# Four graph-network layers on one core: copies, first products, activations and update products of the dense stage moved one round apart, masks of the running sums in 16 bit

## The chip, the cores and the metric

The kernel runs on one core of a Trainium2 chip. The metric is the device time of one execution in microseconds (us). The program is written by hand: each engine (TensorE, ScalarE, VectorE, GpSimdE and SyncE; PE, ACT, DVE, POOL and SP in the profile) has its own stream of instructions and waits on semaphores.

## What is computed

`x` is 100000 x 96 in fp32, there are 50000 edges sorted by `dst`, and four layers follow each other, each as `x = x + layer(relu(layernorm(x)))`. Cut to what matters:

```python
# layer 0 (edges touch only some nodes; for every node:)
update = gelu(concat(h, aggregated) @ uW1 + ub1) @ uW2 + ub2
x = x + layernorm(h + update) * ln_g + ln_b
# layer 1
x = x + relu(concat(h, m) @ Wu1 + bu1) @ Wu2 + bu2
# layer 2: segment mean of (h[src] @ W + b) by dst
# layer 3: three normalised graph convolutions of h, each relu(m @ W + b)
```

`aggregated` and `m` are sums of messages over the edges that end in a node. They are zero for most nodes.

## The kernel before

The work is done in stages, one after another: tables of the edges (0 to about 509 us), the **dense stage**, the edge stage of layer 0 (e0), that of layer 1 (e1), and four convolution stages (conv 0 to 3). The dense stage computes layers 0 and 1 for all nodes as if they had no edges. The later stages correct the nodes that have some.

**Dense stage.** It works on 196 groups of 512 nodes (`NG`). `pipelined(engine, n, stages)` (L107) writes the loop of each engine: in round i it calls each listed function with the group i minus the function's lag, in the order of the list. The lag is the number behind each name. All engines execute their own list strictly in order, but PE may load weights early. What follows is the path of one group, with lines:

- SP loads 512 rows of `x` into `xd`. DVE `mom_x` takes their moments (L1207, `mv<-xd`).
- DVE `roots` (L1160 to L1182, eleven small instructions) turns the moments of three groups at three places of the path into `rstd` and `nmr`. It is the last of each DVE round, and one such batch serves three readers on ACT: `norm1` (this round's new group), `norm_y` and `norm2` (older groups).
- ACT `norm1` writes `hd` (L701, four instructions). PE `tr1` (L895) transposes it into PSUM bank 0. ACT `evac1` (L746) copies that to `hdT`. PE `z1` (L888, `bank<-hdT,uw`) writes the first product to bank 1. ACT `gelu1` (L751) writes `u1`. PE `out1` (L908 and L909, 16 instructions in all) adds the update to the group in PSUM.
- DVE `mom_y` (L1207, `mv<-bank`) takes the moments of that PSUM bank, ACT `norm_y` (L736) normalises it into `yg`, DVE `times_g` (L1226), `plus_x` (L1234) and `plus_b` (L1239) make the new row `xn`, and `mom_z` (L1207, `mv<-xn`) takes its moments.
- ACT `norm2` writes `hs` (L701), PE `tr2` (L916) transposes it into bank 3, ACT `evac2` (L757) copies it, PE `z2` (L888, `bank<-hsT,wu`) makes the first product of layer 1 in bank 4, ACT `relu2` (L762) writes `v1`, PE `out2` (L928) the update product, DVE `finish_x` (L1251) and `finish_o` (L1258) the results.

Banks 0, 1, 3 and 4 are single. So `z1` of group j waits for `gelu1` of group j - 1, and `z2` for `relu2` of the group before. `out1` and `out2` alternate between two banks each.

**Running sums.** In e0, e1 and the convolution stages DVE adds messages along the sorted edges with `tensor_tensor_scan` (L1293): the carry is multiplied by a mask `goes`, 1 where an edge has the same `dst` as the one before and 0 elsewhere. SP loads the mask of 512 edges from DRAM, the same for every partition (L504, L535).

**Queues.** In the e and conv stages POOL gathers rows with indirect DMAs (L610), eight or four instructions for each group of 512 edges. In the dense stage it gathers four small pieces in each round (`got`).

Of the kernel before, what the change touches and what calls it, by code (L numbers as in the profile page):

```python
# [6 lines left out]
F16 = mybir.dt.float16  # L7
I32 = mybir.dt.int32
# [3 lines left out]
P = 128  # L12
# [5 lines left out]
GE = G * P  # L18
EG = 98
ET = EG * G  # L20
E_PAD = EG * GE
NG = (N + GE - 1) // GE
# [3 lines left out]
HI, LO = 128, 784  # L26
# [24 lines left out]
def need(eng, count, value):  # L51

    sem, base = (count.sem, count.base) if isinstance(count, Count) else (count, 0)
    if not isinstance(value, int) or value > 0:
        eng.wait_ge(sem, value + base)  # L55
# [41 lines left out]
def pipelined(eng, n, stages):  # L97


    most = max(stage[1] for stage in stages)  # L100
    last = max([n + most] + [stage[2] for stage in stages if len(stage) > 2])
    first = (most + 2 * UNROLL - 1) // UNROLL * UNROLL
    turns = (n - 1 - first) // UNROLL

    def step(g):
        for stage, lag, *always in stages:
            if g.turn is not None or (always and g.c < always[0]) or (not always and 0 <= g.c - lag < n):  # L107
                stage(g.shift(-lag))

    for i in range(first):  # L110
        step(Group(None, i))
    with eng.Fori(0, turns) as turn:  # L112
        for c in range(UNROLL):
            step(Group(turn, first + c))
    for i in range(first + turns * UNROLL, last):
        step(Group(None, i))


def build(nc, a, out):
    with ExitStack() as ctx:  # L120
        def sb(name, shape, dt=F32):
            return ctx.enter_context(nc.sbuf_tensor(name, shape, dt))
# [4 lines left out]
        def dram(name, shape, dt=F32):  # L127
            return nc.dram_tensor(name, shape, dt, kind="Internal").ap()
# [1 line left out]

        srcp = dram("srcp", (E_PAD,), I32)
        dstp = dram("dstp", (E_PAD + 2,), I32)
        goes_d = dram("goes_d", (E_PAD,))
        info_d = dram("info_d", (HI * LO, 2))
        t1 = dram("t1", (E_PAD + N, D))
        t2 = dram("t2", (E_PAD + N + E_PAD, D))
# [28 lines left out]
        st_s = sb("st_s", [P, ET], I32)  # L165
        st_d = sb("st_d", [P, ET], I32)
        st_p = sb("st_p", [P, ET], I32)
        st_goes = sb("st_goes", [P, ET])
        edge_pad = sb("edge_pad", [1, 2], I32)
        blk_i = sb("blk_i", [LB, 3, 4, P], I32)  # L170
        cols = sb("cols", [P, 3, ET])
# [23 lines left out]
        hd = sb("hd", [P, 6, G, D])  # L195
        mv = sb("mv", [P, 3, 3, G, 3])
# [17 lines left out]
        v1 = g1  # L214
        per_deg = sb("per_deg", [P, 2, G])
        msg = sb("msg", [P, 2, G, D + 1])
        goes = sb("goes", [P, 3, GE])
        iota_lo_i = goes[:, 0:2, :].rearrange("p s e -> p (s e)")[:, 0:LO].bitcast(I32)
        tanh_g = sb("tanh_g", [D, 2, GE])
        msgT = sb("msgT", [D, 2, GE])  # L220
        drop = sb("drop", [P, 3, G, D])
# [6 lines left out]
        xo = sb("xo", [P, 3, G, D])  # L228
        oo = sb("oo", [P, 3, G, D])
        degi, cum = (xn[0:HI, :, :, :].rearrange("p s c d -> p (s c d)")[:, i * LO:(i + 1) * LO] for i in range(2))  # L230
        has, home = (b[0:HI, :, :, :].rearrange("p s c d -> p (s c d)")[:, 0:LO] for b in (xo, oo))
        dego = hd[0:HI, :, :, :].rearrange("p s c d -> p (s c d)")[:, 0:LO]

        bank = [ctx.enter_context(nc.psum_tensor(f"bank{i}", [P, 512], F32)) for i in range(8)]

        def tok(b, w=D):

            return b[:, 0:G * w].rearrange("p (a c) -> p a c", c=w)
# [40 lines left out]
        def Phase(n, counts, slots):  # L279

            made = {}
            for name, per in counts.items():
                made[name] = so_far(name)
                passed[name] = made[name].base + n * per
            for name, (many, dmas, each) in slots.items():
                made[name] = []
                for k in range(many):
                    made[name].append(so_far(f"{name}{k}"))  # L290
                    passed[f"{name}{k}"] += ended((n + each - 1) // each, many, k, dmas)
            return made

        def more(name, k, by):
# [3 lines left out]
        dn = Phase(NG, dict(norm=1, mx=1, my=1, mz=1, t1=1, r1=1, z1=1, g1=1, u1=1, yx=1, xr=1, x1=1, t2=1, r2=1, z2=1,  # L298
                            g2=1, u2=1, fin=1, oo=1, norm2=1, norm_y=1),
                   dict(x_in=(6, 1, 1), x1_out=(6, 1, 1), x2_out=(3, 1, 1), o_out=(3, 1, 1), idx_in=(2, 1, GT),  # L300
                        got=(2, 2 * GI * GT, GT), kept=(2, 1, GT)))
# [394 lines left out]
        def _(act):  # L696
# [33 lines left out]
            def standard(ph, g, y, lag, q):  # L730

                b = g.shift(lag).at(3)
                need(act, ph["root"], ROOT * (g.j + lag + 1))
                need(act, ph["yx"], g.j - 1)
                for c in range(G):
                    ins = nc.scalar.activation(yg[:, g.at(2), c, :], y[:, c, :], ACT.Identity,  # L736
                                               bias=nmr[:, b, q, c:c + 1], scale=rstd[:, b, q, c:c + 1])
                ins.then_inc(ph["norm_y"].sem, 1)

            def norm_y(g):  # L740
                standard(dn, g, tok(bank[2 + 4 * g.at(2)]), 2, 1)

            def evac1(g):
                need(act, dn["t1"], g.j + 1)
# [19 lines left out]

            act.wait_ge(const_step, 1)
            act.wait_ge(weights_in, 16 * n_weights[0])
            pipelined(act, NG, [(gelu1, 1), (relu2, 5), (norm1, 0), (norm2, 4), (norm_y, 2), (evac1, 0), (evac2, 4)])

            for ph in (e0, e1):
                first = ph is e0  # L770
# [85 lines left out]
        def _(pe):  # L856
# [76 lines left out]
            pe.wait_ge(table_step, 7)  # L933
            pe.wait_ge(const_step, 1)
            pe.wait_ge(idx_step, 1)
            pipelined(pe, NG, [(out1, 1), (out2, 5), (tr1, 0), (tr2, 4), (z1, 0), (z2, 4)])

            need(pe, dn["fin"], NG)
            for ph in (e0, e1):
# [100 lines left out]
        def _(dve):  # L1040
# [106 lines left out]
            def pair_stats(x, into):  # L1147

                for c in range(0, G, 2):
                    ins = nc.vector.bn_stats(into[:, c:c + 2, :].rearrange("p c f -> p (c f)"),  # L1150
                                             x[:, c:c + 2, :].rearrange("p c d -> p d c"))
                return ins
# [34 lines left out]
            def roots_of(ph, readers):  # L1187

                def of_round(g):
                    b = g.at(3)  # L1190
                    roots(mv[:, b, :, :, :].rearrange("p q c f -> p (q c) f"),
                          steps + (rstd[:, b, :, :].rearrange("p q c -> p (q c)"), nmr[:, b, :, :].rearrange("p q c -> p (q c)")),
                          readers(g), ph["root"], ROOT * g.j)
                return of_round

            def upto(g, n, *counts):

                return [(count, value if g.turn is not None else min(value, n)) for count, value in counts]

            def wide(row):  # L1200

                return row.unsqueeze(1).broadcast_to([P, G, D])
# [14 lines left out]
            def mom_y(g):  # L1217
                need(dve, dn["u1"], g.j + 1)
                dve.sem_inc(dve_turn, 1)
                pair_stats(tok(bank[2 + 4 * g.at(2)]), mv[:, g.shift(2).at(3), 1, :, :]).then_inc(dn["my"].sem, 1)  # L1220

            def times_g(ph):
                def times(g):
                    need(dve, ph["norm_y"], g.j + 1)
                    dve.sem_inc(dve_turn, 1)
                    nc.vector.tensor_tensor(yx[:], yg[:, g.at(2), :, :], wide(rows[:, 0, :]), ALU.mult)\  # L1226
                        .then_inc(ph["yx"].sem, 1)
                return times
# [30 lines left out]
                    .then_inc(dn["oo"].sem, 1)  # L1259

            def dense_state(g):
                return upto(g, NG, (dn["norm"], g.j - 2), (dn["norm_y"], g.j - 4), (dn["norm2"], g.j - 6),
                            (dn["mx"], g.j + 1), (dn["my"], g.j - 1), (dn["mz"], g.j - 3))

            dve.wait_ge(info_out, 16)
            pipelined(dve, NG, [(times_g(dn), 4), (finish_x, 7), (plus_x, 4), (finish_o, 7), (plus_b, 4), (mom_x, 0),
                                (mom_y, 2), (mom_z, 4), (roots_of(dn, dense_state), 0, NG + 4)])
            for s in range(3):
                need(dve, dn["x2_out"][s], ended(NG, 3, s))
                need(dve, dn["o_out"][s], ended(NG, 3, s))  # L1270
# [213 lines left out]
```

## Time and profile before

| | us |
|---|---|
| median of 3 runs | 6881.36 (6865.93 to 6893.16) |
| the profiled execution's own time | 6877.96 |
| its span, first to last instruction | 6876.1 |
| PE busy | 4438.8 (65%) |
| DVE busy | 3951.5 (57%) |
| ACT busy | 3522.4 (51%) |
| POOL busy | 4259.0 (62%) |

No engine is busy all the time, since the stages have different limits. The busy shares are therefore to be read for each stage, and in a stage by the rounds of its loop: how long a round takes, and which wait ends last in it.

### The profile page before, as it was taken

The page shows a single profiled execution, that of the slowest core. Times are in us where ns is not written, and L with a number is a line of the kernel's source. Part 1 is how long each engine was busy: PE and PEld are TensorE (multiplying, and loading weights), DVE is VectorE, ACT ScalarE, POOL GpSimd, SP SyncE. Part 2 cuts the span into 40 slices and gives each one's busy share as a digit, 9 for nine tenths or more (in the row PEclk, how much of TensorE's full clock was granted, in tenths as well). Part 3 has the DMA queues.
Part 4 walks back from the last instruction along what each step waited for, and adds up shares of the span by engine and source line. Part 5 has one row for each costly group of instructions (what it writes and reads, how often), then busy time and mean ns, then how long its engine had stood idle before and what let it go on. Part 6 is the DMA issues. An engine that isn't in the chain of part 4 may idle for free. (4 is left out here: it accounts for less than half of the span.)

```text
span 6876.1 us, 104878 instructions
## 1 busy us (share of the span) xinstructions
PE 4438.8 (65%) x19614; PEld 2908.5 (42%) x19614; DVE 3951.5 (57%) x12722; ACT 3522.4 (51%) x8822; POOL 4259.0 (62%) x4323
## 2 busy tenths in 40 slices
PE   5768888888886777776887776554555555322222
PEld 2225566555663333333444443444444444222222
DVE  5667777777775666665555554666666344322222
ACT  6987887888885776775555553222222222111110
POOL 0005454555546777775777776775775776677777
PEclk9998988999887888887888887555555555555555
DMA  0003333333332333332444444665554899433332
GB/s 16 0 5 85 102 102 97 102 102 102 102 98 73 77 78 75 76 75 68 118 119 116 119 118 103 161 160 141 123 129 120 119 126 127 79 76 78 79 84 66
DMA packets 958039, 652.70 MB, mean 95 GB/s; under 512 B 730453, under 2 KB 834785, under 8 KB 957946
## 3 DMA queue, kind: packets, MB, share of 16 engines
q1 hardware_dynamic: 819962, 483.05, 25.0%
q0 software_dynamic: 137984, 168.67, 16.2%
q8 instruction: 27, 0.44, 0.0%
q14 instruction: 66, 0.54, 0.0%
HBM read 420.24 MB, written 232.62 MB: 95 GB/s over the span
## 5 line engine op out<-in xcount | busy, mean ns | idle before, releaser
L610 POOL DMA_INDIRECT got<-info_d,idx x784 | 776.8, 991 | 1258.6 <-issue 732.5
L610 POOL DMA_INDIRECT xs<-t,idx x1176 | 1110.8, 945 | 502.4 <-issue 347.7
L1031 PE MATMUL bank<-w,aggT 96*128 96x96 f32 (+1 forms) x3136 | 773.9, 428 | 470.5 <-DVE aggT L1293 470.4
L1024 PE MATMUL bank<-ident,msg 128*96 128x128 f32 (+1 forms) x1568 | 424.3, 426 | 991.3 <-ACT msg L848 819.7
L1031 PEld LDWEIGHTS bank<-w,aggT 96*128 96x128 f32 (+1 forms) x3136 | 703.5, 329 | 581.8 <-issue 500.7
L610 POOL DMA_INDIRECT xs<-c,idx x784 | 748.3, 954 | 314.9 <-issue 233.1
L848 ACT ACTIVATE msg<-xs,now 128x96 f32<-128x96 f32 x784 | 229.3, 363 | 1297.3 <-DMA xs<-c,idx 679.3
L1024 PEld LDWEIGHTS bank<-ident,msg 128*96 128x96 f32 (+1 forms) x1568 | 290.1, 218 | 1052.0 <-ACT msg L848 678.8
L1293 DVE TENSOR_TENSOR_SCAN aggT<-goes,aggT,bank 96x512 f32<-96x512 f32 (+1 forms) x490 | 621.2, 1268 | 135.0 <-DMA goes<-goes_d 63.1
L701 ACT ACTIVATE hd<-xd,nmr,rstd 128x96 f32<-128x96 f32 x1568 | 599.1, 454 | 27.0 <-DVE nmr L1182 27.0
L610 POOL DMA_INDIRECT xs<-in_x_dram,idx x392 | 473.3, 1207 | 173.9 <-issue 119.2
L1207 DVE BATCH_NORM_STATS2 mv<-xs 128x6 f32<-128x192 f32 x392 | 122.9, 355 | 752.4 <-DMA xd<-in_x_dram,idx 353.9
L1435 DVE SCALAR_TENSOR_TENSOR y<-bank,now,rows 128x96 f32<-128x96 f32 x392 | 97.3, 311 | 702.3 <-PE bank L1031 702.3
L687 POOL DMA_INDIRECT out_dram<-xn,idx_out x392 | 390.4, 996 | 119.4 <-issue 119.1
L610 POOL DMA_INDIRECT xd<-in_x_dram,idx x392 | 386.8, 987 | 119.4 <-issue 119.4
L610 POOL DMA_INDIRECT xd<-t,idx x392 | 370.0, 944 | 119.4 <-issue 119.4
L1435 DVE SCALAR_TENSOR_TENSOR xn<-bank,now,rows 128x96 f32<-128x96 f32 x784 | 194.5, 311 | 395.1 <-PE bank L1031 358.6
L875 PE MATMUL bank<-xd,hot_hi 128*128 128x392 f16 x1568 | 324.8, 329 | 124.0 <-ACT hot_hi L713 115.7
L949 PE MATMUL bank<-ident,hs 128*128 128x128 f32 (+1 forms) x784 | 151.4, 325 | 376.3 <-ACT hs L701 374.8
L701 ACT ACTIVATE hs<-xs,nmr,rstd 128x96 f32<-128x96 f32 x784 | 300.3, 455 | 174.0 <-DVE nmr L1182 173.8
L1093 DVE TENSOR_SCALAR xd<-iota_lo,lo_of 128x784 f16<-128x784 f16 x784 | 297.0, 421 | 143.6 <-PE bank L875 143.5
L888 PE MATMUL bank<-hdT,uw 96*96 96x512 f32 x392 | 249.1, 721 | 179.2 <-ACT hdT L746 179.2
(189 smaller groups left out, 10722.2 us busy)
## 6 DMA issues: line engine op xcount, KB each, us to landing
goes<-goes_d SPq DMA_DIRECT2D x392, 256.0 KB
t<-xo SPq DMA_DIRECT2D x392, 192.0 KB, 3.5
t<-xn SPq DMA_DIRECT2D x294, 192.0 KB, 2.3
xd<-in_x_dram SPq DMA_DIRECT2D x196, 192.0 KB, 2.4
out_dram<-oo SPq DMA_DIRECT2D x196, 192.0 KB
goes<-goes_d SPq DMA_DIRECT2D x196, 192.0 KB
xd<-t SPq DMA_DIRECT2D x196, 192.0 KB, 4.0
c<-xn SPq DMA_DIRECT2D x196, 192.0 KB, 3.7
```

What stands on the lines that cost most here:

```text
L610: nc.gpsimd.indirect_dma_start(out=into, out_offset=None, in_=table, in_offset=bass.IndirectOffsetOnAxis(ap=indices, axis=0)).then_inc(don ...
L687: nc.gpsimd.indirect_dma_start(out=out[:, :], out_offset=bass.IndirectOffsetOnAxis(ap=idx_out[:, half(g), col + c:col + c + 1], axis=0), i ...
L701: ins = nc.scalar.activation(into[:, c, :], x[:, c, :], ACT.Relu, bias=nmr[:, b, q, c:c + 1], scale=rstd[:, b, q, c:c + 1])
L848: ins = nc.scalar.activation(msg[:, g.at(2), c, 0:D], xs[:, g.at(6), c, :], ACT.Relu, scale=scale[:, col + c:col + c + 1])
L875: ins = nc.tensor.matmul(bank[1 + 2 * which + side][0:HI, 0:SIDE], hot_hi[:, g.at(2), which, 0:HI], hot_lo[:, g.at(2), which, side * SIDE: ...
L888: nc.tensor.matmul(into, w, x, start=True, stop=True).then_inc(done.sem, 1)
L949: ins = nc.tensor.transpose(bank[0][0:w, c * P:(c + 1) * P], hs[:, g.at(3), c, 0:w], ident[:])
L1024: ins = nc.tensor.transpose(bank[g.at(2)][0:m, c * P:(c + 1) * P], msg[:, g.at(2), c, 0:m], ident[:])
L1031: ins = nc.tensor.matmul(tok(bank[2 + g.at(2)], m)[:, c, :], aggT[0:m, g.at(3), c * P:(c + 1) * P], w2[:] if k == 0 else w3[:, k - 1, :], ...
L1093: nc.vector.tensor_scalar(hot_lo[:, g.at(2), which, :], iota_lo[:], lo_of[:, which, bass.ds(g.j, 1)], None, ALU.is_equal).then_inc(hot, 1)
L1293: nc.vector.tensor_tensor_scan(aggT[0:m, s, :], goes[0:m, s, :], source(g), aggT[0:m, before, GE - 1:GE], ALU.mult, ALU.add)\
L1435: ins = nc.vector.scalar_tensor_tensor(out=to, in0=u[:, c, 0:D], scalar=now[:, half(g), 1, col + c:col + c + 1], in1=rows[:, 1 + k, :], op ...
```

## The change

In the dense stage `evac1`, `z1`, `evac2` and `z2` are called one round later than before (lags 1 and 5, which were 0 and 4), and so are `gelu1`, `out1`, `relu2` and `out2` (lags 2 and 6, which were 1 and 5). `mom_y` and `norm_y` have lag 3, which was 2. `norm1`, `tr1`, `norm2`, `tr2`, `times_g`, `plus_x`, `plus_b`, `mom_z` and `finish_x` keep their lags. Each engine's list is put in another order too. Apart from the dense stage, the mask is kept in 16 bit, in DRAM and in SBUF, and the integers from which a constant is made lie in another buffer, since the mask's has become too small.

```diff
-        goes_d = dram("goes_d", (E_PAD,))
+        goes_d = dram("goes_d", (E_PAD,), F16)
...
-        st_goes = sb("st_goes", [P, ET])
+        st_goes = sb("st_goes", [P, ET], F16)
...
-        goes = sb("goes", [P, 3, GE])
-        iota_lo_i = goes[:, 0:2, :].rearrange("p s e -> p (s e)")[:, 0:LO].bitcast(I32)
+        goes = sb("goes", [P, 3, GE], F16)
...
+        iota_lo_i = hd[:].rearrange("p s c d -> p (s c d)")[:, 1024:1024 + LO].bitcast(I32)
...
-                standard(dn, g, tok(bank[2 + 4 * g.at(2)]), 2, 1)
+                standard(dn, g, tok(bank[2 + 4 * g.at(2)]), 3, 1)
...
-            pipelined(act, NG, [(gelu1, 1), (relu2, 5), (norm1, 0), (norm2, 4), (norm_y, 2), (evac1, 0), (evac2, 4)])
+            pipelined(act, NG, [(evac1, 1), (evac2, 5), (gelu1, 2), (relu2, 6), (norm_y, 3), (norm1, 0), (norm2, 4)])
...
-            pipelined(pe, NG, [(out1, 1), (out2, 5), (tr1, 0), (tr2, 4), (z1, 0), (z2, 4)])
+            pipelined(pe, NG, [(z1, 1), (z2, 5), (out1, 2), (out2, 6), (tr1, 0), (tr2, 4)])
...
-                pair_stats(tok(bank[2 + 4 * g.at(2)]), mv[:, g.shift(2).at(3), 1, :, :]).then_inc(dn["my"].sem, 1)
+                pair_stats(tok(bank[2 + 4 * g.at(2)]), mv[:, g.shift(3).at(3), 1, :, :]).then_inc(dn["my"].sem, 1)
...
-                return upto(g, NG, (dn["norm"], g.j - 2), (dn["norm_y"], g.j - 4), (dn["norm2"], g.j - 6),
-                            (dn["mx"], g.j + 1), (dn["my"], g.j - 1), (dn["mz"], g.j - 3))
+                return upto(g, NG, (dn["norm"], g.j - 2), (dn["norm_y"], g.j - 5), (dn["norm2"], g.j - 6),
+                            (dn["mx"], g.j + 1), (dn["my"], g.j - 2), (dn["mz"], g.j - 3))
...
-            pipelined(dve, NG, [(times_g(dn), 4), (finish_x, 7), (plus_x, 4), (finish_o, 7), (plus_b, 4), (mom_x, 0),
-                                (mom_y, 2), (mom_z, 4), (roots_of(dn, dense_state), 0, NG + 4)])
+            pipelined(dve, NG, [(finish_x, 7), (mom_y, 3), (finish_o, 7), (mom_x, 0), (times_g(dn), 4), (plus_x, 4),
+                                (plus_b, 4), (mom_z, 4), (roots_of(dn, dense_state), 0, NG + 4)])
```

How the instructions stand on ACT, in a steady round of the dense stage, before:

```order
L701 ACTIVATE hd<-xd,nmr,rstd 128x96 x4
L701 ACTIVATE hs<-xn,nmr,rstd 128x96 x4
L736 ACTIVATE yg<-bank,nmr,rstd 128x96 x4
L746 ACTIVATE hdT<-bank 96x512
L757 ACTIVATE hsT<-bank 96x512
L751 ACTIVATE u<-bank,bias 96x512
L762 ACTIVATE g<-bank,bias 96x512
```

And with the change (the first row is the first of a round here):

```order
L746 ACTIVATE hdT<-bank 96x512
L757 ACTIVATE hsT<-bank 96x512
L751 ACTIVATE u<-bank,bias 96x512
L762 ACTIVATE g<-bank,bias 96x512
L736 ACTIVATE yg<-bank,nmr,rstd 128x96 x4
L701 ACTIVATE hd<-xd,nmr,rstd 128x96 x4
L701 ACTIVATE hs<-xn,nmr,rstd 128x96 x4
```

`norm_y` (L736) has moved ahead of `norm1` and `norm2` (L701). The copies, which before stood behind the norms of their own groups, now serve the groups that were transposed a round earlier, and the norms end the round. On PE the order around the ring is the one of before (`z1`, `z2`, `out1`, `out2`, `tr1`, `tr2`), only for other groups.

On DVE, in a steady round of the dense stage, before:

```order
L1182 SCALAR_TENSOR_TENSOR nmr<-mv,rstd 128x12
L1226 TENSOR_TENSOR yx<-yg,rows 128x384
L1251 TENSOR_TENSOR xo<-xn,bank 128x384
L1234 TENSOR_TENSOR xn<-yx,xd 128x384
L1258 TENSOR_TENSOR oo<-xo,relu_b 128x384
L1239 TENSOR_TENSOR xn<-xn,rows 128x384
L1207 BN_STATS mv<-xd 128x6 x2
L1207 BN_STATS mv<-bank 128x6 x2
L1207 BN_STATS mv<-xn 128x6 x2
L1160 TENSOR_SCALAR var<-mv 128x12
```

And with the change:

```order
L1182 SCALAR_TENSOR_TENSOR nmr<-mv,rstd 128x12
L1251 TENSOR_TENSOR xo<-xn,bank 128x384
L1207 BN_STATS mv<-bank 128x6 x2
L1258 TENSOR_TENSOR oo<-xo,relu_b 128x384
L1207 BN_STATS mv<-xd 128x6 x2
L1226 TENSOR_TENSOR yx<-yg,rows 128x384
L1234 TENSOR_TENSOR xn<-yx,xd 128x384
L1239 TENSOR_TENSOR xn<-xn,rows 128x384
L1207 BN_STATS mv<-xn 128x6 x2
L1160 TENSOR_SCALAR var<-mv 128x12
```

`finish_x` (L1251) and `mom_y` (L1207, `mv<-bank`), the two that read what PE wrote, have moved to the head of the round. `times_g`, `plus_x`, `plus_b` and `mom_z`, each of which reads what the one before wrote, now stand next to each other.

## Rows read from the trace of the kernel before

**Rows 1.** Windows (us; busy PE, PEld, DVE, ACT, POOL; clock; DMA; GB/s): dense stage, e1.

```profile
565.10:2089.00 1523.90, 1285.90 (x6923) 905.44 (x6921) 1161.14 (x4238) 1251.36 (x3074) 745.35 (x752) 0.88 0.33 101
...
3270.00:4240.00 970.00, 774.62 (x3484) 454.79 (x3483) 508.40 (x1720) 517.26 (x1154) 714.35 (x757) 0.87 0.47 117
```

**Rows 2.** Instructions that write `oo` (min/median/max ns, first and last start).

```profile
L1258 DVE TENSOR_TENSOR oo<-xo,relu_b x196: 544/551/558, 565.1 to 2089.0; 128x384 f32<-128x384 f32 x196
```

**Rows 3.** Timeline of PE, one dense round (start us, us, name, idle before).

```profile
1523.72 1.10 PE L888 MATMUL bank<-hdT,uw 96*96 96x512 f32 x2 [1.12 <-ACT hdT L746]
1524.66 1.02 PE L888 MATMUL bank<-hsT,wu 96*96 96x512 f32 x2
1525.59 0.46 PE L908 MATMUL bank<-uw,u 97*128 97x96 f32 x2
...
1527.45 1.06 PE L928 MATMUL bank<-wu,g 97*128 97x96 f32 x8
1528.35 0.60 PE L895 MATMUL bank<-ident,hd 128*96 128x128 f32 x4
1529.31 0.64 PE L916 MATMUL bank<-ident,hs 128*96 128x128 f32 x4 [0.36 <-ACT hs L701]
1531.07 1.10 PE L888 MATMUL bank<-hdT,uw 96*96 96x512 f32 x2 [1.12 <-ACT hdT L746]
```

**Rows 4.** Timeline of ACT, the same round.

```profile
1524.86 0.68 ACT L751 ACTIVATE u<-bank,bias 96x512 f32<-96x512 f32 x1 [0.71 <-PE bank L888]
1525.72 0.68 ACT L762 ACTIVATE g<-bank,bias 96x512 f32<-96x512 f32 x1 [0.17 <-PE bank L888]
1526.30 1.53 ACT L701 ACTIVATE hd<-xd,nmr,rstd 128x96 f32<-128x96 f32 x4
1527.73 1.53 ACT L701 ACTIVATE hs<-xn,nmr,rstd 128x96 f32<-128x96 f32 x4
1529.17 1.37 ACT L736 ACTIVATE yg<-bank,nmr,rstd 128x96 f32<-128x96 f32 x4
1530.43 0.59 ACT L746 ACTIVATE hdT<-bank 96x512 f32<-96x512 f32 x1
1530.91 0.59 ACT L757 ACTIVATE hsT<-bank 96x512 f32<-96x512 f32 x1
```

**Rows 5.** Timeline of DVE, the same round.

```profile
1523.92 0.17 DVE L1182 SCALAR_TENSOR_TENSOR nmr<-mv,rstd 128x12 f32<-128x12 f32 x1
...
1524.53 0.55 DVE L1251 TENSOR_TENSOR xo<-xn,bank 128x384 f32<-128x384 f32 x1
1524.99 0.55 DVE L1234 TENSOR_TENSOR xn<-yx,xd 128x384 f32<-128x384 f32 x1
...
1527.77 0.63 DVE L1207 BATCH_NORM_STATS2 mv<-bank 128x6 f32<-128x192 f32 x2 [0.75 <-PE bank L909]
1528.31 0.61 DVE L1207 BATCH_NORM_STATS2 mv<-xn 128x6 f32<-128x192 f32 x2
1529.06 0.27 DVE L1160 TENSOR_SCALAR var<-mv 128x12 f32<-128x12 f32 x1
...
1531.21 0.17 DVE L1182 SCALAR_TENSOR_TENSOR nmr<-mv,rstd 128x12 f32<-128x12 f32 x1
```

**Rows 6.** Timeline of DVE, an early dense round without `finish_x` and `finish_o`.

```profile
541.72 0.56 DVE L1234 TENSOR_TENSOR xn<-yx,xd 128x384 f32<-128x384 f32 x1
542.32 0.56 DVE L1239 TENSOR_TENSOR xn<-xn,rows 128x384 f32<-128x384 f32 x1
```

**Rows 7.** Timeline of PE, a dense round at the lower clock.

```profile
1505.33 1.92 PE L928 MATMUL bank<-wu,g 97*128 97x96 f32 x8
1507.03 1.06 PE L895 MATMUL bank<-ident,hd 128*96 128x128 f32 x4
```

**Rows 8.** Instructions that write `aggT`, and what DVE was idle for before them (us, times).

```profile
L1293 DVE TENSOR_TENSOR_SCAN aggT<-goes,aggT,msgT x98: 1265/1273/1299, 2127.8 to 3214.2; 96x512 f32<-96x512 f32 x98
...
  DMA goes<-goes_d: 63.1, 26
```

## The prediction

> **What bounds the kernel now.** I read the windows first, to see which stage the change touches and what limits it. The dense stage's steady part, 1523.9 us, has PE busy 1285.9 us, ACT 1251.4 us and DVE 1161.1 us, at a mean granted clock of 0.88 [rows 1]. No engine there is full, so the limit is a ring of waits. The first and the last `finish_o` stand at 565.1 and 2089.0 us and there are 196 of them [rows 2], so a round takes 1523.9 / 195 = 7.815 us on average. In e1 POOL is busy 714 us of 970 and its 757 instructions have small gaps between them [rows 1]. The mask can give little there unless it delays a gather.
>
> Then I read one round of the dense stage at the full clock, engine by engine. `z1` starts at 1523.72 and again at 1531.07 us, so the round is 7.35 us [rows 3]. ACT works through the round with two pauses, 0.71 us before `gelu1` and 0.17 us before `relu2` [rows 4]. PE pauses 1.12 us before `z1`, waiting for the copy on ACT, and 0.36 us before `tr2` [rows 3]. DVE pauses 0.75 us before `mom_y`, for `out1` [rows 5]. **The ring that closes is ACT's own**: the seven steps of its list plus the trip copy, `z1`, `gelu1`. The reader should see that only 0.88 us of a round is pause on ACT, which is the most that taking this trip off ACT's path can give: 7.35 - 0.88 = 6.47 us.
>
> At the lower clock (1.2 GHz; the full one is 2.4) PE is the limit. `out2` to `tr1` takes 0.90 us at the full clock [rows 3] and 1.70 us at the lower [rows 7], 1.89 times as long. PE's work in a full-clock round is 7.35 - 1.12 - 0.36 = 5.87 us, so 11.1 us at the lower clock. A mean of 0.88 means 24% of the time at the lower one. From 1/7.815 = 0.76/7.35 + 0.24/T comes T = 9.8 us for a round there, 0.88 of 11.1, because the low stretches are short and rounds straddle them.
>
> **The change, part by part.** Nothing is added or removed in the dense loop. PE, ACT and DVE issue the same instructions, SP's list is untouched, and so are its DMAs and POOL's gathers. What changes is which round serves which group, and the order inside a round.
>
> *The trip is taken off ACT's path.* `gelu1` now reads a product that PE made in the round before. ACT's 0.71 and 0.17 us go. ACT alone could do 6.47 us.
>
> *What is late next: PE's ring.* `z1` in a PE round still needs bank 1 free, and it is freed by the `gelu1` of the same ACT round, which stands behind `evac2`. `evac2` waits for `tr2`, the last step of PE's round before. So PE's 5.87 us are followed by 0.48 us for the copy, 0.68 us for `gelu1` [rows 4] and two handovers of 0.05 us (the copy of 1530.43 ends at 1531.02 and `z1` starts at 1531.07). That is 7.13 us. By this ring alone the change would still gain 0.22 us a round.
>
> *What is later still: a ring over all three engines that spans two rounds.* I follow it from the end of `roots` in DVE round i. (1) ACT round i now does `norm_y`, `norm1`, `norm2` in this order: 1.26 + 1.43 + 1.53 = 4.22 us [rows 4]. (2) PE `tr2` of round i, 0.64 us [rows 3]. (3) ACT round i+1: `evac2` 0.48 us, then `gelu1` 0.68 us. (4) PE round i+1: `z1` 0.94, `z2` 0.93, `out1` 1.86, `out2` 1.06, together 4.79 us [rows 3]. (5) DVE round i+2 begins with `finish_x`, whose `out2` was made in PE round i+1 (lags 7 and 6), and then `mom_y` (lags 3 and 2). Nothing of that round can pass them. DVE then does `finish_x` 0.46, `mom_y` 0.54, `finish_o` 0.46, `mom_x` 0.54 [rows 5]. (6) `times_g`, `plus_x` and `plus_b` each feed their neighbour now. Where they stood so in an early round one took 0.60 us from start to start [rows 6] against 0.46 us between neighbours that don't depend on each other [rows 5]: 3 x 0.60 = 1.80 us. (7) `mom_z` 0.75 us and `roots` 2.15 + 0.17 = 2.32 us [rows 5]. Steps 5 to 7 are 6.87 us. With five handovers of 0.05 us the ring is 4.22 + 0.64 + 1.16 + 4.79 + 6.87 + 0.25 = 17.93 us for two rounds, **8.97 us a round**.
>
> I tried the same count on the kernel before. There `mom_y` stands near the end of DVE's round, `finish_x` reads what PE made two rounds earlier, and `z1` doesn't wait behind `tr2` and `evac2`. The ring is `norm1` 1.43, `norm2` 1.44, `norm_y` 1.26, copy 0.59, `z1` 1.10, `gelu1` 0.68, from `out1` to `mom_y` 2.18, `mom_y` 0.54, `mom_z` 0.75, `roots` 2.32 and four handovers, 12.49 us, which leaves 14.70 - 12.49 = 2.21 us of slack in two rounds. `nmr` ends at 1524.09 and ACT takes it up at 1526.30 us, 2.21 us later [rows 4, 5]. The count describes the old loop, and in the new one it has 17.93 us to fit into 14.70.
>
> *Behind the waiting instructions.* On ACT all three norms wait at `norm_y`; behind them stand the copies. On DVE everything waits at `finish_x`, the loads' release (`plus_x`) among it. SP issues the load two rounds ahead of `mom_x`, which covers it.
>
> *At the lower clock* PE's ring is 11.1 + 1.26 = 12.4 us and the long one (17.93 + 0.89 x 5.43) / 2 = 11.4 us. PE's ring counts; by the 0.88 of before a round there takes 10.9 us.
>
> *How often the clock is low.* PE's work falls from 80% to 5.87 / 8.97 = 65% of a full-clock round, with nearly all of the pause between `out2` and the next `z1`. The nearest rows are the dense stage with 0.88 and e1 with 0.87 [rows 1], so I keep 24%. The ends are none of the time and half of it. A mean round is then 1 / (0.76/8.97 + 0.24/10.9) = 9.37 us, times 195 = 1827 us, **303 us more** than 1524. The first rounds and the drain are not counted apart.
>
> *The masks.* The bytes of 588 loads are halved. DVE waited 63.1 us for a mask, in 26 scans [rows 8], and the scans of e0 took 1273 ns each for 512 elements. From below the gain is nothing (nothing gets longer: the same packets with fewer bytes). From above it is the 63.1 us, and if a 16-bit mask halved the 98 scans of e0, 62 us more. A scan costs 2.49 ns an element and an addition on DVE 0.55 us for 384, 1.43 ns [rows 5, 8]; one operand in 16 bit with the others in 32 has no row here. I take 15 us, near the lower end, since the wait is in one stage alone and its rounds have POOL's pace beside it. The Trainium skill (DVE: opcode table, instruction layouts, handler registers and perf-mode slots, section on datapath and trigger behaviour) says that the built-in scan runs at half throughput because its result goes back to an earlier stage for each element. By that rule the 62 us are out and the upper bound is 63; the trace's ratio of element costs fits it.
>
> **Sum.** 6877.96 + 303 - 15 = 7166 us for the profiled execution. The median of the runs shown is 3.4 us above that execution's time, so I forecast 7165 to 7170 us and write 7168.
>
> **The rivals.**
>
> *Faster: the long ring doesn't close.* If one of its handovers reaches a round further than I read, 17.93 us spread over three rounds, 5.98 us, and PE's ring of 7.13 us decides. The point is where the long ring takes less than 7.13 us a round. With 9.8 us at the lower clock the mean is 1 / (0.76/7.13 + 0.24/9.8) = 7.62 us, 1486 us in all, 38 us saved: 6878 - 38 - 15 = 6825, with the median's 3 us 6828 us, 0.8% faster. For it speaks only that the change takes a real pause off ACT. Against it speaks the check on the old loop, which came out to a hundredth. Chance 0.08.
>
> *No change: the new order holds the old pace*, because the pauses come out on other engines but the round stays at 7.35 us, and the masks are hidden but for the 15 us: 6866 us. The same if the dense part did not do what it says. Chance 0.04.
>
> *Slower still: the clock goes with the pauses.* PE's pauses before `tr1`, `tr2` and `z1` come in one row, 3.1 us in 8.97. If half of the time is spent at the lower clock, the mean is 1 / (0.5/8.97 + 0.5/12.4) = 10.4 us, 2030 us in all, +506: 7370 us; if all of it, 195 x 12.4 = 2418 us, +894: 7760 us. For it: the pauses are longer than before. Against it: e1 keeps 0.87 although PE waits for POOL there [rows 1]. The Trainium skill (TensorE: Matmul & The Clock Gate, section on the second failure mode, depth-cycling in PSUM) says that short idle times between groups of matmuls, as banks are cycled, make the clock swing between its levels. By that rule this rival is the likelier the more pauses a round has; the trace shows such swings already before. Chance 0.08.
>
> **How the numbers follow.** The forecast has what is left, 0.80. Its own range: with the clock always full 195 x 8.97 = 1749 us, +225, and all 125 us of the masks, 6981 us; with 36% low at 12.4 us, a round of 9.96 us, +418: 7284 us. The range is 6990 to 7320 us. It leaves out the faster and the unchanged case and most of the clock's, nearly 2 in 10. A measurement of this kernel tells about 0.5%, 34 us, from no change. Faster by more: 0.08. Within: 0.04. Slower: 0.88.
>
> **What would show it.** Right: in the dense stage DVE's longest wait stands before `finish_x` (L1251, released by `out2`, L928) and not before `mom_y`; ACT waits before `norm_y` (L736) for `nmr`, about 1.5 to 2 us a round; PE waits before `z1` for `gelu1` (L751); full-clock rounds take about 9.0 us; the scans take 1.27 us as before. Wrong: rounds of 7.1 to 7.4 us, ACT without a wait for `nmr`, or a stage that ends near 2090 us.

## The result and the profile after

The changed kernel takes **7584.3 us** (median of 4 runs, 7577.9 to 7589.8) against 6881.2 us, a ratio of 1.102 with a 95% interval from 1.100 to 1.105. The direction was forecast, the size was not: 7168 us in a range that ended at 7320.

The page of the changed kernel, its engines and the row of the granted clock in 40 slices:

```profile
span 7584.4 us, 104907 instructions
...
PE 5023.4 (66%) x19614; PEld 3381.1 (45%) x19614; DVE 3987.7 (53%) x12722; ACT 3519.3 (46%) x8822; POOL 4252.2 (56%) x4323
...
PEclk9985555656555658888878888855555555555555
```

PE is busy 585 us longer with the same 19614 instructions (5023.4 us for 4438.8). The row of the granted clock is low from the fourth slice to the fifteenth, which is the dense stage. The first and last `finish_o`, to be set beside [rows 2]:

```profile
L1258 DVE TENSOR_TENSOR oo<-xo,relu_b x196: 540/542/558, 570.9 to 2810.2; 128x384 f32<-128x384 f32 x196
```

The steady part now takes 2239.3 us for 1523.9, +715.4. What stands before it is 5.8 us longer, and from its end to the end of the span it is 4774.2 us for 4787.1, -12.9. The sum, 708.3 us, is the difference of the spans (7584.4 - 6876.1). A round takes 2239.3 / 195 = 11.48 us for 7.81.

Windows of the changed kernel: the steady part, one stretch at the full clock, and the low one behind it (columns as in [rows 1]):

```profile
570.90:2810.20 2239.30, 1851.67 (x6920) 1367.76 (x6920) 1202.48 (x4239) 1259.34 (x3072) 728.07 (x748) 0.59 0.23 69
...
1574.10:1584.20 10.10, 5.30 (x34) 3.82 (x33) 8.73 (x28) 6.05 (x16) 7.05 (x7) 1.00 0.27 79
1584.40:1655.90 71.50, 63.43 (x220) 47.13 (x219) 34.76 (x127) 39.60 (x97) 23.81 (x24) 0.50 0.22 67
```

The mean clock is 0.59: 82% of the stage at 1.2 GHz, where it was 24%. The longest waits of DVE, ACT and PE in the steady part (us in total, times, longest; only POOL, which is off this path, waits longer in sum):

```profile
DVE xo L1251 <- PE bank L928: 900.4, 193, 8.5
ACT yg L736 <- DVE nmr L1182: 518.0, 167, 4.7
...
PE bank L888 <- ACT u L751: 255.6, 190, 1.4
```

These are the three handovers that the prediction named for the new rings: DVE at `finish_x` for `out2`, ACT at `norm_y` for `nmr`, PE at `z1` for `gelu1`. PE at the end of the full-clock stretch and in the low one:

```profile
1575.51 1.07 PE L888 MATMUL bank<-hdT,uw 96*96 96x512 f32 x2 [1.35 <-ACT u L751]
...
1582.76 0.65 PE L895 MATMUL bank<-ident,hd 128*96 128x128 f32 x4 [2.66 <-ACT hd L701]
1584.19 1.09 PE L916 MATMUL bank<-ident,hs 128*96 128x128 f32 x4 [0.79 <-ACT hs L701]
1586.62 1.99 PE L888 MATMUL bank<-hdT,uw 96*96 96x512 f32 x2 [1.35 <-ACT u L751]
...
1598.44 1.99 PE L888 MATMUL bank<-hdT,uw 96*96 96x512 f32 x2 [1.35 <-ACT u L751]
```

In this stretch at the full clock PE waits 1.35, 2.66 and 0.79 us and is busy 5.3 us of 10.1; then the clock falls. At the lower clock PE is continuously busy but for 1.35 us before each `z1`, and a round is 1598.44 - 1586.62 = 11.82 us. No round of the steady part lies at the full clock from `z1` to `z1`. In the trace's record of the clock the steady part has 38 stretches at the full clock, each of 10.2 us, and 37 low ones between them, of 24 to 106 us with a median of 48. Before, the low ones were all of 10.2 us, 33 of them (a 34th begins 20 us before the last `finish_o` and runs on past it), and the full ones had a median of 38.

The scans keep their duration (median 1274 ns for 1273), so the mask's width changed nothing there on DVE:

```profile
L1293 DVE TENSOR_TENSOR_SCAN aggT<-goes,aggT,msgT x98: 1265/1274/1286, 2850.0 to 3944.0; 96x512 f32<-96x512 f16 x98
```

### The profile page after: what moved, and what is told of

Read it like the earlier page. It is cut to its first block and busy times, and to the rows that moved or that the text cites. A ratio compares the mean times of both kernels' runs of the same rounds, so it can differ in the third digit from the quotient of the medians.

```text
span 7584.4 us, 104907 instructions
## 1 busy us (share of the span) xinstructions
PE 5023.4 (66%) x19614; PEld 3381.1 (45%) x19614; DVE 3987.7 (53%) x12722; ACT 3519.3 (46%) x8822; POOL 4252.2 (56%) x4323
## 5 line engine op out<-in xcount | busy, mean ns | idle before, releaser
L1293 DVE TENSOR_TENSOR_SCAN aggT<-goes,aggT,bank 96x512 f32<-96x512 f16 (+1 forms) x490 | 621.0, 1267 | 86.9 <-DMA goes<-goes_d 29.1
L701 ACT ACTIVATE hd<-xd,nmr,rstd 128x96 f32<-128x96 f32 x1568 | 600.9, 461 | 27.2 <-DVE nmr L1182 27.2
L1251 DVE TENSOR_TENSOR xo<-xn,bank 128x384 f32<-128x384 f32 x196 | 108.6, 554 | 902.5 <-PE bank L928 901.8
L736 ACT ACTIVATE yg<-bank,nmr,rstd 128x96 f32<-128x96 f32 x784 | 273.5, 429 | 604.6 <-DVE nmr L1182 527.6
L888 PE MATMUL bank<-hdT,uw 96*96 96x512 f32 x392 | 356.4, 1008 | 264.5 <-ACT u L751 263.8
L1207 DVE BATCH_NORM_STATS2 mv<-xs 128x6 f32<-128x192 f32 x392 | 122.8, 355 | 773.3 <-DMA xd<-in_x_dram,idx 362.0
L908 PEld LDWEIGHTS bank<-uw,u 97*128 97x128 f32 x1568 | 414.9, 307 | 190.8 <-issue 187.9
L909 PE MATMUL bank<-ident,hdT 96*128 96x96 f32 x1568 | 460.3, 393 | 0.0
L908 PE MATMUL bank<-uw,u 97*128 97x96 f32 x1568 | 450.5, 387 | 0.0
```

What stands on the lines that cost most here:

```text
L701: ins = nc.scalar.activation(into[:, c, :], x[:, c, :], ACT.Relu, bias=nmr[:, b, q, c:c + 1], scale=rstd[:, b, q, c:c + 1])
L888: nc.tensor.matmul(into, w, x, start=True, stop=True).then_inc(done.sem, 1)
L908: nc.tensor.matmul(to, u1[:, g.at(2), e], uw2[:], start=True, stop=False)
L909: ins = nc.tensor.matmul(to, hdT[0:D, g.at(3), e], ident[0:D, 0:D], start=False, stop=True)
L1293: nc.vector.tensor_tensor_scan(aggT[0:m, s, :], goes[0:m, s, :], source(g), aggT[0:m, before, GE - 1:GE], ALU.mult, ALU.add)\
```

## The experiments

Theory A: the ring over three engines and two rounds makes PE pause, and the pauses bring the clock down. Its rivals: it is PE's pause before `z1` alone (B), or the clock is low for another reason (C).

**e1: the masks alone**, in the kernel before.

```diff
-        goes_d = dram("goes_d", (E_PAD,))
+        goes_d = dram("goes_d", (E_PAD,), F16)
...
-        st_goes = sb("st_goes", [P, ET])
+        st_goes = sb("st_goes", [P, ET], F16)
...
-        goes = sb("goes", [P, 3, GE])
+        goes = sb("goes", [P, 3, GE], F16)
...
```

> The kernel before with the 16-bit masks alone; the dense loop is the old one. All theories: the dense stage stays at 1524 us between the first and the last finish_o. By the traces of the two kernels, what follows the dense stage took 4787 us before (2089 to 6876) and 4774 us after (2810 to 7584), so the masks are worth about 13 us: 6868 us, ratio 0.998. Rival: the masks cost or gain something that the dense stage's length hides; then the ratio is outside 0.995 to 1.000. Scans stay at 1.27 us.

Measured: 6867.9 us, ratio 0.9974 (0.9960 to 0.9987). The masks gain about 0.26%, 18 us (9 to 28 by the interval). In its trace DVE waits 31.0 us for masks, in 13 scans, for 63.1 in 26 [rows 8]. The dense stage, whose code is the one of before, takes 1534.8 us there for 1523.9, so two traces of the same loop can differ by 11 us. The whole loss is the dense loop's.

**e2: DVE's list with `finish_x` and `mom_y` late**, in the changed kernel.

```diff
-            pipelined(dve, NG, [(finish_x, 7), (mom_y, 3), (finish_o, 7), (mom_x, 0), (times_g(dn), 4), (plus_x, 4),
-                                (plus_b, 4), (mom_z, 4), (roots_of(dn, dense_state), 0, NG + 4)])
+            pipelined(dve, NG, [(times_g(dn), 4), (mom_x, 0), (plus_x, 4), (plus_b, 4), (mom_z, 4), (finish_x, 7),
+                                (mom_y, 3), (finish_o, 7), (roots_of(dn, dense_state), 0, NG + 4)])
```

> The changed kernel with DVE's dense list reordered: times_g, mom_x, plus_x, plus_b, mom_z first, then finish_x, mom_y, finish_o, roots. It takes some 3.0 us of work out of the stretch from out2 to roots. Theory A (the ring over three engines and two rounds makes PE pause at the full clock, and the pauses bring the clock down): the ring is (17.93 - 3.0) / 2 = 7.5 us, the pauses of PE shrink to about 1.6 us a round, the granted clock in the dense stage goes back to 0.8 or more, the stage to 1500 to 1600 us and the whole to 6850 to 6950 us. Theory B (the pause before z1, behind evac2 and gelu1, is what holds the clock low, whatever DVE does): the clock stays near 0.59, rounds near 11.5 us, the whole near 7580 us.

Measured: 7379.0 us, ratio 1.071 (1.068 to 1.074), clock 0.60, a mean round of 2060.7 / 195 = 10.57 us. 205 us come back, so the ring through DVE costs something, but the clock did not rise and the time is 429 us above theory A's range. B had the clock right and the time 201 us too high. The waits show a ring that I had overlooked:

```profile
DVE yx L1226 <- ACT yg L736: 304.7, 192, 1.6
```

`times_g` now leads the round and needs `norm_y`, which needs the roots just before it: 1.6 us of wait in every round. Two successive rounds at the full clock take 7.18 and 8.10 us (`z1` at 1359.61, 1366.80 and 1374.90 us). The pause of 1.35 us before `z1` at the lower clock is as in the changed kernel, and so is the median of the low stretches, 44 us. They are uneven, though: 7 of 25 last 3.4 us and 10 last 116 us or more.

**e3: `gelu1` and `relu2` before `evac2`** on ACT.

```diff
-            pipelined(act, NG, [(evac1, 1), (evac2, 5), (gelu1, 2), (relu2, 6), (norm_y, 3), (norm1, 0), (norm2, 4)])
+            pipelined(act, NG, [(evac1, 1), (gelu1, 2), (relu2, 6), (evac2, 5), (norm_y, 3), (norm1, 0), (norm2, 4)])
```

> The changed kernel with ACT's dense list reordered: evac1, gelu1, relu2, evac2 and then the norms. z1 no longer waits behind tr2 and evac2. Theory A: the long ring only falls to 8.6 us at the full clock, PE still pauses for some 2.7 us of it, and the clock stays low (0.55 to 0.65); a round at the lower clock is PE's own 11.1 us, so the stage takes 2100 to 2180 us and the whole 7440 to 7520 us. Theory B: the pause before z1 goes, the clock rises over 0.8, rounds take 9 us, the whole 7100 to 7200 us.

Measured in one timed run: 7416.8 us, clock 0.57. That is theory A's clock, and its time but for 23 us. B as stated is out, but the pause before `z1` was cut to 0.50 us at the lower clock, not removed: `gelu1` still stood behind `evac1`. A round that lies wholly at the lower clock takes 10.97 us.

```profile
1230.96 1.99 PE L888 MATMUL bank<-hdT,uw 96*96 96x512 f32 x2 [0.50 <-ACT u L751]
```

**e4: five matmuls more** on PE in each round, into unused columns of a free bank. Nothing reads them.

```diff
+            def fill(g):
+                for c in range(5):
+                    nc.tensor.matmul(bank[2 + 4 * g.shift(1).at(2)][:, 384:512], ident[:], ident[:], start=True, stop=True)
...
-            pipelined(pe, NG, [(z1, 1), (z2, 5), (out1, 2), (out2, 6), (tr1, 0), (tr2, 4)])
+            pipelined(pe, NG, [(z1, 1), (z2, 5), (out1, 2), (out2, 6), (tr1, 0), (tr2, 4), (fill, 4)])
```

> The changed kernel with five more matmuls (ident by ident, 128 x 128, into unused columns of a free PSUM bank) on PE after tr2 in each dense round, where PE waits for evac2 and gelu1. They compute nothing that is used. Theory A, with the clock following PE's pauses: the pause before z1 is filled, the clock rises to 0.8 or more, full-clock rounds take 9.0 us by the long ring (which the filler isn't on), the stage takes 1780 to 1900 us and the whole 7130 to 7250 us. Theory C (the clock is low for another reason than PE's pauses, and PE's own ring at the lower clock sets the round): the filler adds its 2.8 us at the lower clock less the 1.3 us pause, the round goes from 11.8 to 13.3 us and the whole to 7870 us.

Measured in one timed run: 7205.1 us, 379 us *less* than the changed kernel, with more work on PE. The window of its steady part:

```profile
568.20:2434.00 1865.80, 1493.23 (x8860) 1187.87 (x8860) 1202.06 (x4239) 1234.17 (x3073) 754.40 (x751) 0.85 0.27 82
```

The clock is 0.85, a mean round 9.57 us, and C is out. This run also shows the long ring apart from most of the clock's effect. The stage is 342 us longer than before although PE's clock is about the same (0.85 for 0.88). The prediction had +303 for it. The waits come as a ring over two rounds would bring them: the rounds alternate between 6.8 to 7.8 us and 11.7 to 12.4 us (`z1` at 1308.27, 1315.07 and 1327.50 us, so 19.23 us for two), and DVE waits for `out2` once in two rounds, 99 times for 193:

```profile
DVE xo L1255 <- PE bank L932: 526.3, 99, 6.2
```

(The added lines of `fill` move `finish_x` to L1255 and `out2` to L932.)

**e5, e6 and e7** ran together where the kernel before took 9201.8 us for 6881. In the dense stage of the traces of e6 and e7, PE, ACT and DVE stand still together for about 10 us in every 37.5 and 34 us while POOL's gathers go on; in e5 PE stands still for 7 us in every 39. There is no trace of the kernel before from there. I conclude nothing from them and repeated all three. They divide theory A: by A1 a pause of PE at the lower clock keeps the clock low, by A2 only the pauses at the full clock count. Their expectations, and what came out:

> The changed kernel with ACT's dense list gelu1, evac1, relu2, evac2 and then the norms: against the run with evac1, gelu1, relu2, evac2 only one pair is swapped. In that run PE still paused 0.50 us before z1 in each round at the lower clock (evac1 and gelu1 after tr1, less tr2), and the low stretches were mostly 27 to 102 us long; in the changed kernel the pause is 1.35 us and they were 24 to 106 us, in the kernel before it is nearly none and they were 10.2 us each. Theory A1 (a short pause of PE at the lower clock is what keeps it there): here the copy of evac1 hides under tr2, PE runs through, low stretches are 10 us or less, the clock is 0.75 or more, the stage 1750 to 1850 us and the whole 7090 to 7190 us. Theory A2 (only the pauses at the full clock count, which the long ring of 8.6 us makes): they are as long as in that run, so the clock stays near 0.57 and the whole near 7420 us.

9501.9 us.

> Both reorderings: ACT with gelu1 first, DVE with finish_x, mom_y, finish_o after mom_z. The run with the late DVE list alone showed a ring I had overlooked: times_g now leads DVE's round and waits 1.59 us for norm_y, which waits for the roots just before; that is some 8.2 us a round at the full clock. Theory A1: PE has no pause at the lower clock, low stretches are 10 us, full rounds 8.2 us, the clock 0.8 or more, the stage about 1700 us and the whole about 7040 us. Theory A2: the clock is as in the late-DVE run, 0.60, the whole 7350 to 7400 us.

9373.4 us.

> A version meant to have no ring above an engine's own work: ACT with gelu1 first; times_g, plus_x, plus_b, mom_z, norm2, tr2 one round later than in the changed kernel (lag 5), evac2 and z2 6, relu2 and out2 7, finish_x 8 and behind roots, finish_o 9. Theory A1 with the count of rings: from roots over the norms, gelu1, evac1, z1, z2, out1 to mom_y and roots is 12.4 us in two rounds, so DVE's own work of 6.6 to 6.8 us sets the full-clock round; PE pauses less than 1 us in it and not at all at the lower clock, the clock is 0.85 or more, the stage 1350 to 1430 us and the whole 6700 to 6780 us, ratio 0.975 to 0.985. Theory A2 says the same of the clock here. Rival D (a later reader of xn, the loads or the stores close another ring): rounds of 7.3 us or more, no gain over the kernel before.

9149.7 us, ratio 0.993 (0.991 to 0.996).

**e9: `gelu1` first** (the kernel of e5), one pair swapped against e3.

```diff
-            pipelined(act, NG, [(evac1, 1), (gelu1, 2), (relu2, 6), (evac2, 5), (norm_y, 3), (norm1, 0), (norm2, 4)])
+            pipelined(act, NG, [(gelu1, 2), (evac1, 1), (relu2, 6), (evac2, 5), (norm_y, 3), (norm1, 0), (norm2, 4)])
```

> The kernel of e5 again: one pair swapped against e3 (gelu1 before evac1). Theory A1 (a pause of PE at the lower clock keeps it there, and here there is none): low stretches of 10 us or less, clock 0.75 or more, the whole 7090 to 7190 us. Theory A2 (only the pauses at the full clock count, and they are those of e3): clock near 0.57, the whole near 7420 us.

Measured in one timed run: 7418.6 us, clock 0.66. Each theory got half. The low stretches fell from a median of 41 us (up to 102) in e3 to 13.7 us (up to 37.5): in a round wholly at the lower clock PE now runs without a pause, and such a round takes 10.33 us. Two `z1` without a pause before them, and the next `tr1`:

```profile
1059.26 2.02 PE L888 MATMUL bank<-hdT,uw 96*96 96x512 f32 x2
...
1069.67 1.35 PE L888 MATMUL bank<-hdT,uw 96*96 96x512 f32 x2
...
1078.30 1.09 PE L895 MATMUL bank<-ident,hd 128*96 128x128 f32 x4 [3.77 <-ACT hd L701]
```

But the full-clock stretches stayed at a median of 6.8 us. In about every second round PE still pauses 2.3 to 4.1 us before `tr1`, waiting for `hd` (3.77 us in the last row), and two rounds take 21.3 us by the long ring. So the stage took 2048.6 us for 2072.0 in e3, 23 us less, and the whole no less. (Beside e9 the kernel before took 6907 us, beside e3 6881, so a gain of some 25 us by the order is not excluded.)

**e10: `gelu1` first and DVE's late list** (the kernel of e6).

> The kernel of e6 again: the late DVE list and gelu1 first. Theory A1: low stretches of 10 us, full rounds of 8.2 us by the ring roots, norm_y, times_g, clock 0.8 or more, the whole about 7040 us. Theory A2: the clock as with the late DVE list alone, 0.60, the whole 7350 to 7400 us.

Measured in one timed run: 7072.5 us, clock 0.74 in the steady part, low stretches of 10.2 us in the median, full ones of 13.7. A1's time is met to 32 us; its clock of 0.8 or more is not. Against e2, the order of ACT's list alone is worth 307 us. Against the changed kernel, with its long ring, the same order gave 166 us (e9).

**e8: every ring that I had counted opened** (the kernel of e7). `gelu1` is first on ACT, the second layer's chain and `times_g` to `mom_z` come one more round later, `finish_o` two, and `finish_x` stands behind `roots`. Buffer places and waits that follow from the lags are left out here.

```diff
-            pipelined(act, NG, [(evac1, 1), (evac2, 5), (gelu1, 2), (relu2, 6), (norm_y, 3), (norm1, 0), (norm2, 4)])
+            pipelined(act, NG, [(gelu1, 2), (evac1, 1), (relu2, 7), (evac2, 6), (norm_y, 3), (norm1, 0), (norm2, 5)])
...
-            pipelined(pe, NG, [(z1, 1), (z2, 5), (out1, 2), (out2, 6), (tr1, 0), (tr2, 4)])
+            pipelined(pe, NG, [(z1, 1), (z2, 6), (out1, 2), (out2, 7), (tr1, 0), (tr2, 5)])
...
-            pipelined(dve, NG, [(finish_x, 7), (mom_y, 3), (finish_o, 7), (mom_x, 0), (times_g(dn), 4), (plus_x, 4),
-                                (plus_b, 4), (mom_z, 4), (roots_of(dn, dense_state), 0, NG + 4)])
+            pipelined(dve, NG, [(times_g(dn), 5), (mom_x, 0), (plus_x, 5), (finish_o, 9), (plus_b, 5), (mom_z, 5),
+                                (mom_y, 3), (roots_of(dn, dense_state), 0, NG + 5), (finish_x, 8)])
```

> The kernel of e7 again. In that call the kernel before took 9202 us where it takes 6881 us elsewhere, and PE stood still for about 10 us in every 34, in all kernels; nothing is concluded from it. As for e7: Theory A1 expects full-clock rounds near 7 us or less, short low stretches (about 10 us), a clock of 0.85 or more in the dense stage, 6700 to 6800 us and a ratio of 0.975 to 0.985. Rival D (another ring) expects full-clock rounds of 7.3 us or more and no gain over the kernel before.

Measured: **6656.4 us, ratio 0.964** (0.962 to 0.965) to the kernel before, which took 6907.3 us beside it. It beats both kernels. Its steady part, and PE in one round of it:

```profile
572.30:1858.60 1286.30, 1130.80 (x6881) 782.64 (x6880) 1160.67 (x4214) 1212.61 (x3047) 731.57 (x748) 0.99 0.39 119
```

```profile
1003.47 1.10 PE L888 MATMUL bank<-hdT,uw 96*96 96x512 f32 x2 [0.41 <-ACT hdT L746]
...
1008.99 0.64 PE L916 MATMUL bank<-ident,hs 128*96 128x128 f32 x4 [0.28 <-ACT hs L701]
1010.04 1.10 PE L888 MATMUL bank<-hdT,uw 96*96 96x512 f32 x2 [0.41 <-ACT hdT L746]
```

A round is 6.57 us here and 6.60 us on average. PE's pauses are 0.28 and 0.41 us in this round (the longest before the last rounds is 0.59 us), and the clock stays full from 558.1 to 1838.1 us; it falls in the last three rounds, where the loop runs empty. ACT is busy 1212.6 us of the 1286.3, near the 6.47 us a round that the prediction gave for ACT alone. The expectation was too careful: it left up to 15% for the lower clock.

The kernels side by side (steady part of the dense stage; the pause is PE's longest one in a round at the lower clock, in e4 before `tr2`, in the others before `z1`; stretches are medians; all in us but the clock; e3, e4, e9 and e10 have one timed run each):

| kernel | pause at the lower clock | low stretch | full stretch | clock | mean round | time |
|---|---|---|---|---|---|---|
| before | none | 10.2 | 38 | 0.88 | 7.81 | 6881 |
| changed | 1.35 | 48 | 10.2 | 0.59 | 11.48 | 7584 |
| e2 | 1.35 | 44 | 17 | 0.60 | 10.57 | 7379 |
| e3 | 0.50 | 41 | 6.8 | 0.57 | 10.63 | 7417 |
| e4 | 0.35 | 6.8 | 13.7 | 0.85 | 9.57 | 7205 |
| e9 | none | 13.7 | 6.8 | 0.66 | 10.51 | 7419 |
| e10 | none | 10.2 | 13.7 | 0.74 | 8.75 | 7072 |
| e8 | low only at the end | - | 1280 | 0.99 | 6.60 | 6656 |

## Why the prediction was wrong

**Right: where it waits.** All three handovers of the new rings stand among the longest waits of their engines, in the places named. ACT's wait for `nmr` is longer than the 1.5 to 2 us that the prediction gave: 518.0 us in 167 rounds, 3.1 us each. The trip was taken off ACT's path and the loop did not get faster by it.

**Right, as far as it can be read: the long ring's size.** It was put at 17.93 us for two rounds at the full clock and +303 us for the stage at the clock of before. e4, where the clock is 0.85, has 19.1 us for two rounds and +342 us. No run shows this ring at an unbroken full clock, so the round of 9.0 us that was to be the sign is not measured. The check on the old loop, which came out to a hundredth, compared sums of intervals with the same trace: it showed that the chain was complete, not what the new one would cost.

**Right: the masks, nearly.** 15 us were taken; e1 measured about 18 (9 to 28), and behind the dense stage 12.9 us are gone. The bound of 62 us for faster scans fell: 1274 ns for 1273.

**Wrong: "How often the clock is low".** The step kept 24% from the nearest rows, the dense stage itself and e1 [rows 1]. It was 82%. Put into the prediction's own formula, 82% gives 1 / (0.18/8.97 + 0.82/12.4) = 11.6 us a round and 2262 us for the stage, where 2239 were measured, so this term alone explains the miss to 23 us. With e4 as the divide, +342 us of the 715 go to the ring at a clock of about 0.85, and the other 373 us to the clock. This is an estimate, since the parts do not simply add up: the late DVE list alone gives back 205 us (e2), `gelu1` first alone 166 us (e9), both together 512 us (e10). The step failed in its argument and not only in a figure. It asked which share of time comes with how much pausing, as if one number answered. The traces show two questions. What PE does at the *full* clock goes with how soon it falls: in the changed kernel pauses of 1.35, 2.66 and 0.79 us stand in a stretch that ends after 10.2 us, in e8 pauses of at most 0.6 us, until the last rounds, in one of 1280 us. What PE does at the *lower* clock goes with how soon it rises: with no pause before `z1` the low stretches have medians of 7 to 14 us, with 0.50 or 1.35 us in each round of 41 to 48 us. The prediction had computed that second pause (the 1.26 us of PE's own ring) and used it only as time, 12.4 us a round. The measured round there is 11.82 us, and without the pause 10.33 us (e9), so PE's own work at the lower clock, put at 11.1 us, was too high. Nor did the prediction see that the pauses at the full clock would be longer than the ring's own 3.1 us: in the round from 1575.51 to 1586.62 us PE waits 2.66, 0.79 and 1.35 us, 4.8 in all. Probably the ring still carries steps there that were done at the lower clock; no run shows this apart.

The row that speaks against my step was in the trace of before. PE's first dense rounds, which have fewer matmuls, pause twice at the lower clock. The clock is low from 498.8 to 556.8 us, 47 us of it in the dense stage, while the 33 later low stretches, in which PE runs on without such pauses, are 10.2 us long. In the trace of the kernel before:

```profile
539.43 2.02 PE L888 MATMUL bank<-hdT,uw 96*96 96x512 f32 x2 [0.68 <-ACT hdT L746]
542.23 0.74 PE L908 MATMUL bank<-uw,u 97*128 97x96 f32 x2 [0.77 <-ACT u L751]
547.49 2.02 PE L888 MATMUL bank<-hdT,uw 96*96 96x512 f32 x2 [0.68 <-ACT hdT L746]
```

**The rival that came true** is the clock's, priced at 7370 us for half of the time and 7760 us for all. 7584 lies between them, as 82% does. It had a chance of 0.08, and the range stopped short of it. The rule of the Trainium skill cited beside it (TensorE: Matmul & The Clock Gate, the second failure mode) agrees with the trace in its direction: with pauses between the groups of matmuls the clock swings, 38 times up in this stage, and with pauses of at most 0.6 us in e8 it does not. I gave it less weight than e1's mean.

**What stays open.** No run varies PE's pause in small steps, so its part in the clock is shown by the order of these kernels and not as a size. e2 has low stretches of 3.4 us and of 116 us with the same pause of 1.35 us, and why is not known. That the full-clock stretches of e9 (6.8 us) are shorter than those of e10 (13.7 us) fits the longer pauses before `tr1` in e9; no run changes those pauses alone.

## What to carry to other kernels

To move work one round apart takes a wait off one engine, and may close a ring through the others: follow the chain from the last instruction of a round, over each engine's list and each lag, to the same instruction again, and divide by the rounds that it spans. Do it for every reader that has come to the head of a list (`finish_x`, `times_g`), and open each ring that is longer than the busiest engine's own work, as e8 did.

Where PE's clock is not full all the time, count PE's pauses twice, at the full clock and at the lower one. In this kernel a pause of 0.50 or 1.35 us before `z1` in each round at the lower clock came with low stretches of 41 to 48 us in the median. Removing the 1.35 us where the long ring was shorter too (e10 against e2) was worth 307 us in 195 rounds, 1.57 us each.

## What the runs showed that I had not expected

- More work on PE made the kernel faster: five idle matmuls a round (e4) take it from 7584 to 7205 us.
- One swapped pair on ACT changes the low stretches from 41 to 14 us in the median and leaves the time at 7417 and 7419 us (e3, e9): two rounds take 21.3 us by the long ring in e9.
- With pauses of 0.28 and 0.41 us in a round the clock stayed full for 1280 us (e8), where with 0.36 and 1.12 us [rows 3] it fell 33 times before the loop ran empty.
- In the dense stage of e7, PE, ACT and DVE stood still together for about 10 us in every 34 us, in e6 in every 37.5 us, and the kernel before, timed beside them, was a third slower as well. The cause is not known.
